# Two convolution layers: two input buffers, and sums of squares issued group by group

## The reference, cut to what matters

```python
def _hconv(x, w, b):
    return _project(_expmap0(_conv3x3(_logmap0(x), w, b)))
def _hbn(x, gamma, beta): ...      # log map, batch norm, exp map, project
out = _hconv(out_of_group_norm, w1, b1)   # first conv_layer
out = _hbn(out, g1, beta1); out = _hrelu(out)
out = _hconv(out, w2, b2)                 # second conv_layer
```

## Time and profile before

| | us |
|---|---|
| median of 3 runs | 12048.74 (12042.55 to 12057.85) |
| the profiled execution, whole | 12020.56 |
| its span, first to last instruction | 12018.7 |
| PE / DVE / ACT busy | 9492.6 (79%) / 9408.9 (78%) / 8396.4 (70%) |

### The profile page before, as it was taken

The page is one execution under the profiler, slowest core; times in us unless marked ns, Lnnn a source line. Parts: engine busy times, 40 slices in busy tenths (PEclk is TensorE's granted clock), DMA queues, the critical chain, the costliest instruction groups (busy, mean ns, idle before and its releaser), DMA issues. The chain is left out here.

```text
span 12018.7 us, 360844 instructions
## 1 busy us (share of the span) xinstructions
PE 9492.6 (79%) x152226; PEld 4623.4 (38%) x152226; DVE 9408.9 (78%) x10971; ACT 8396.4 (70%) x5579; POOL 298.0 (2%) x132
## 2 busy tenths in 40 slices
PE   0888778885657799868888888888888888887787
PEld 0333223333435666533333333333333333333444
DVE  6677656657776666579999999999999999998776
ACT  0555455555531133279999999999999999998777
POOL 0000000000004500000000000000000000000000
PEclk9999999997879899989999999999999999998899
DMA  7888788886642244355555555555555555554555
GB/s 265 236 239 239 208 228 246 244 229 243 269 195 64 69 153 153 127 100 105 104 102 108 102 106 104 107 102 105 102 109 101 107 101 107 104 107 75 178 176 162
DMA packets 1165596, 1796.78 MB, mean 149 GB/s; under 512 B 124832, under 2 KB 929824, under 8 KB 1094048
## 3 DMA queue, kind: packets, MB, share of 16 engines
q1 hardware_dynamic: 1164320, 1777.49, 58.1%
HBM read 701.15 MB, written 402.65 MB: 92 GB/s over the span
## 5 line engine op out<-in xcount | busy, mean ns | idle before, releaser
L1886 DVE SCALAR_TENSOR_TENSOR grown_ex<-ratio,ex 128x2048 f32<-128x2048 f32 x1024 | 2330.8, 2286 | 250.9 <-PE out L2019 107.4
L2019 PE MATMUL out<-ex,kan_basis 32*32 32x512 f32 x32768 | 1451.1, 654 | 637.8 <-DVE z L1868 359.6
L1764 ACT ACTIVATE ex<-ex 128x2048 f32<-128x2048 f32 x1024 | 1925.8, 1899 | 4.1
L2019 PE MATMUL out<-grown_ex,kan_basis 32*32 32x512 f32 x32768 | 1563.8, 645 | 51.7 <-DVE grown_ex L1886 50.8
L547 PE MATMUL conv<-uc,w 128*32 128x512 f32 x12288 | 1442.8, 611 | 21.0 <-DMA uc<-u 21.0
L1760 ACT ACTIVATE ex<-kin,offset 128x2048 f32<-128x2048 f32 x512 | 1013.2, 1991 | 68.8 <-PE out L2019 60.5
L456 ACT ACTIVATE v<-conv,cb 128x512 f32<-128x512 f32 x512 | 350.5, 684 | 789.8 <-PE conv L547 786.4
L2019 PEld LDWEIGHTS out<-ex,kan_basis 32*32 32x32 f32 x32768 | 396.6, 107 | 1113.5 <-issue 1045.1
L2019 PEld LDWEIGHTS out<-grown_ex,kan_basis 32*32 32x32 f32 x32768 | 541.3, 107 | 673.5 <-issue 582.4
L2138 DVE TENSOR_TENSOR d<-xt 128x2313 f32<-128x2313 f32 (+2 forms) x256 | 622.1, 2494 | 215.3 <-PE acc L2195 215.0
L2195 PE MATMUL acc<-d,weights 32*32 32x512 f32 x16384 | 667.1, 632 | 113.3 <-issue 109.6
(11 more groups left out here) (284 smaller groups left out, 17527.2 us busy)
## 6 DMA issues: line engine op xcount, KB each, us to landing
uc<-u SPq DMA_DIRECT2D x2048, 129.0 KB, 2.8
xt<-in_x SPq DMA_DIRECT2D x128, 1024.0 KB, 7.3
t<-v SPq DMA_DIRECT2D x128, 1024.0 KB, 5.8
back_k<-ku SPq DMA_DIRECT2D x1024, 128.0 KB
xt<-in_x SPq DMA_DIRECT2D x32, 2048.0 KB, 7.8
xt<-t SPq DMA_DIRECT2D x64, 1024.0 KB, 7.6
tt<-t SPq DMA_DIRECT2D x64, 1024.0 KB, 10.8
x<-x SPq DMA_DIRECT2D x64, 1024.0 KB, 4.9
```

The lines of the kernel that those rows point to most:

```text
L1764: a.activation(ex[:, j], ex[:, j], ACT.Exp, scale=-1.0).then_inc(exps, 1)
L1886: v.scalar_tensor_tensor(grown_ex[:, j % 2], ratio[:], LARGEST, ex[:, j], ALU.min, ALU.mult).then_inc(grown, 1)
L2019: last = m.matmul(out[rows(i), g, :], k["kan_basis"][rows(g), kind - 1, n, :], base[rows(g), cols(i)], start=(n == 0), stop=(n == BASES - ...
```

## The change

- `xt` gets a second buffer. The load of band `n+1` is issued in round `n`, where that of band `n` was; it waits for the same count of `normed` and `squared` as before. Band 0 is loaded ahead of the rounds. Semaphores `loaded` are split by parity.
- ACT does `square(n, 0)` and `square(n, 1)` earlier: between the evacuations of groups 1, 2 and 3 of half 0 instead of behind them.
- PE does `sum_squares(n)` ahead of `fill_u(n-1, 0)`, no longer ahead of `fill_u(n-1, 2)`.
- `sum_out` is cut into one piece for each group `k`: 2 blocks, two of the four column quadrants, instead of 8 blocks. A piece stands behind the convolution of the next group. `sqv` is four banks, one for each `k`, instead of two halves.
- The convolution of group 0 of half 0 moves from the start of round `n+1` to the end of round `n`, between groups 3 of half 1's convolution and the last piece of `sum_out`. Its evacuation moves with it. `roots` waits for the last piece.
- Some small tiles of DVE are overlaid to make room, and with that the wait for `spread_u` stands earlier in `factors_u`.
- The order of DVE and of SP is as before, apart from that.

```diff
-        xt = sb("xt", [P, HALVES, HALO, COLS])
+        xt = sb("xt", [P, 2, HALVES, HALO, COLS])
-        sqv = sb("sqv", [P, HALVES, TILE])
+        sqv = sb("sqv", [P, 4, BANK])
...
-            def load(r):
+            def load(r, parity):
                 for h in range(HALVES):
-                    wait_both(sp, normed, 2 * (r - 1) + h + 1, squared, 2 * (r - 1) + h + 1)
+                    wait_both(sp, normed, 2 * (r - 2) + h + 1, squared, 2 * (r - 2) + h + 1)
...
+            load(0, 0)
             def round_(n, parity):
-                if exists(n):
-                    load(n)
+                if exists(n + 1):
+                    load(n + 1, 1 - parity)
...
             def evacuate(r, parity, h, groups):
                 if groups[0] == 0:
                     wait_past(act, stored[parity][h], 8 * (r - parity))
                     wait_past(act, measured[h], r - 1)
-                    wait_past(act, summed_out, 2 * (r - 1) + h + 1)
                 for k in groups:
+                    wait_past(act, summed_out, (2 * r + h) * 4 + k - 3)
                     act.wait_ge(conv_ready, (2 * r + h) * 4 + k + 1)
...
             def round_(n, parity):                      # ACT
                 if exists(n - 2):
-                    evacuate(n - 2, parity, 0, (0, 1))
+                    evacuate(n - 2, parity, 0, (1,))
+                if exists(n):
+                    square(n, parity, 0)
                 if first and exists(n - 1):
                     logarithms(n - 1)
                 if exists(n - 2):
-                    evacuate(n - 2, parity, 0, (2, 3))
+                    evacuate(n - 2, parity, 0, (2,))
                 if exists(n):
-                    square(n, 0)
-                    square(n, 1)
+                    square(n, parity, 1)
                 if exists(n - 2):
+                    evacuate(n - 2, parity, 0, (3,))
                     evacuate(n - 2, parity, 1, (0, 1))
...
                     evacuate(n - 2, parity, 1, (3,))
+                if exists(n - 1):
+                    evacuate(n - 1, 1 - parity, 0, (0,))
...
+            def sum_out(r, h, k):
+                if h == 0 and k == 0:
                     wait_past(pe, read, r + 2)
+                pe.wait_ge(evacuated, (2 * r + h) * 4 + k + 1)
+                for i in range(2):
+                    b = BAND * h + 4 * (k // 2) + k % 2 + 2 * i
...
             def round_(n, _):                           # PE
                 if exists(n - 2):
-                    convolve(n - 2, 0, (0, 1))
+                    for k in (1, 2, 3):
+                        convolve(n - 2, 0, (k,))
+                        sum_out(n - 2, 0, k - 1)
                 if exists(n - 3):
                     fill_out(n - 3, 0)
                 if exists(n - 2):
-                    convolve(n - 2, 0, (2, 3))
+                    convolve(n - 2, 1, (0,))
+                    sum_out(n - 2, 0, 3)
+                if exists(n):
+                    sum_squares(n)
                 if exists(n - 1):
                     fill_u(n - 1, 0)
                 if exists(n - 2):
-                    convolve(n - 2, 1, (0,))
+                    convolve(n - 2, 1, (1,))
+                    sum_out(n - 2, 1, 0)
                 if exists(n - 1):
                     fill_u(n - 1, 1)
                 if exists(n - 2):
-                    convolve(n - 2, 1, (1,))
-                if exists(n):
-                    sum_squares(n)
+                    convolve(n - 2, 1, (2,))
                 if exists(n - 1):
                     fill_u(n - 1, 2)
                 if exists(n - 2):
-                    convolve(n - 2, 1, (2,))
-                    sum_out(n - 2, 0)
+                    sum_out(n - 2, 1, 1)
                 if exists(n - 3):
                     fill_out(n - 3, 1)
                 if exists(n - 2):
                     convolve(n - 2, 1, (3,))
-                    sum_out(n - 2, 1)
+                    sum_out(n - 2, 1, 2)
+                if exists(n - 1):
+                    convolve(n - 1, 0, (0,))
+                if exists(n - 2):
+                    sum_out(n - 2, 1, 3)
```

More of the change, by code:

```diff
@@ L345, in sem @@
             return net.sem(local, name)
-        loaded, uc_loaded, measured = ([sem(f"{k}{h}") for h in range(2)] for k in ("loaded", "uc_loaded", "measured"))
-        stored = [[sem(f"stored{parity}{h}") for h in range(2)] for parity in range(2)]
+        uc_loaded, measured = ([sem(f"{k}{h}") for h in range(2)] for k in ("uc_loaded", "measured"))
+        loaded, stored = ([[sem(f"{k}{parity}{h}") for h in range(2)] for parity in range(2)] for k in ("loaded", "stored"))
         ready = sem("params")
@@ L361, in rounds @@
                 round_(n, n % 2)
-            with eng.Fori(2, BANDS // 2) as pair:
+            with eng.Fori(2, BANDS // 2 - 1) as pair:
                 for parity in range(2):
                     round_(pair * 2 + parity, parity)
-            for n in range(BANDS, BANDS + 5):
+            for n in range(BANDS - 2, BANDS + 5):
                 round_(n, n % 2)
@@ L495, in sum_squares @@
                     last.then_inc(summed_u, 1)
[L497 to L498 removed]
+            def sum_out(r, h, k):
+                if h == 0 and k == 0:
                     wait_past(pe, read, r + 2)
[L500 to L502 removed]
+                pe.wait_ge(evacuated, (2 * r + h) * 4 + k + 1)
+                for i in range(2):
+                    b = BAND * h + 4 * (k // 2) + k % 2 + 2 * i
                     q4 = QUAD * (b % 4)
[L504 removed]
+                    last = m.matmul(pc[q4:q4 + QUAD, 1, :], c["ones"][:, b // 4, :], sqv[:, k, COLS * i:COLS * i + COLS],
                                     start=(b < 4), stop=(b >= HALVES * BAND - 4), tile_position=(0, q4))
```

69 lines of the change are left out of this document (32 added, 37 removed).

## The result

| | before | after |
|---|---|---|
| median of 4 runs each, us | 12045.65 (12033.58 to 12057.85) | 12286.3 (12271.1 to 12288.09) |
| span of the profiled execution | 12018.7 | 12286.2 |
| start of the layer behind the two convolutions | 2742.6 | 3116.3 |
| round of the first / second convolution layer | 37.4 / 36.5 | 44.25 / 41.5 |

The account below looks back on a forecast made before the run. Chains of handovers, no full engine or DMA, bound each round. Rounds 5.3 and 5.5 us longer, times 31, add 335 us to 12020.6, giving 12356; 28 more for the median gives 12385 us, range 12200 to 12560.

Parts of the forecast that it names:

- The mechanism: Convolution layers: group 0 queued ahead of the last piece puts half 0's `uc` regroup, 12.8 us, into the chain through `roots`.
- the hold: ACT's first evacuation of half 1 waits for `measure(n-4, 1)`; PE stands 2.3 us before its piece, slot 1 behind it.
- The walk: Step-by-step timing of one round from the read of `roots` to the next: 41.1 us first layer, 40.4 second, before clock loss.
- The rival without a hold: ACT not held by the measurement, slot 1 starts 2.35 us earlier: 146 us less, 12240; chance 0.1.
- The clock: Behind PE's 4.4 us wait for `uc` the clock drops, costing 1.6 us a round in both layers, counted once.
- a bound outside the sum: Second clock loss behind the 2.3 us pause before half 1's piece: 99 us more, 12485; with dear pieces, chance 0.14.
- The pieces: Eight `sum_out` pieces on PE at 0.5 us each, six of them in the loop.
- the low end: Pieces at 0.22 us if the next group fills idle quadrants: 104 us less, 12280; chance 0.08.
- The sum of the layers: Rounds 5.3 us longer in the first and 5.5 in the second convolution layer, times 31 rounds: 335 us.
- The untouched layers: Layers behind the two convolutions: no change in their time was priced.
- The rivals for faster and for no change: Faster: waits go, regroup doesn't replace them, 11910, chance 0.06. No change: gains and loop cancel, 12050, chance 0.04.
- break-even: Loop is shorter than before's round only if `u_done` comes under 21.2 us behind `roots` in the first layer, 20.2 second.

Follow-up runs that it names:

- e1: Changed kernel with the convolution of group 0 of half 0 and its evacuation back at the start of the next round: 12162.05 us, ratio 1.0109 to before.
- x8: x5 with group 0 of half 0 and its evacuation put back at the end of the round, ahead of the last `sum_out` piece: 11965.64 us, ratio 0.9939.
- e2: Changed kernel with the second part of `measure(n-4, 1)` on DVE moved ahead of `take_u` slot 0: 12121.31 us, ratio 1.0072 to before.
- p2: Kernel before with the last pass of the loop over bands written out behind the loop, same work and order: 11907.94 us, ratio 0.9893.
- x5: e1 with the slots one group earlier and ACT's squares and PE's `sum_squares` moved later, two input buffers and pieces kept: 11760.05 us, ratio 0.9769 to before.
- x7: x5 with before's single `xt` buffer and its waits instead of two buffers: 11801.78 us, ratio 0.9803 to before.

## Why the prediction was right, point by point

**The mechanism, right, with one loop missing.** Half 0's regroup came into the chain, as forecast, and PE waits for `uc` 4.5 and 4.1 us once a round (forecast 4.4). The chain was drawn through `roots`. e1 cut exactly that link and won 2.6 us in the first layer and 0.2 in the second, where 5.0 were to be explained. What lengthens the rounds of both layers is the way from group 0 to `u_done` in PE's list: in the first 23.2 us before and 31.7 after, in the second 19.5 and 28.6. Before's way had a pause that no row has shown so far, ahead of `fill_out`:

```profile
815.39 1.15 PE L512 MATMUL spread<-factor_out,c_sel 32*128 32x256 f32 x16 [1.73 <-DVE factor_out L602]
```

In the first layer, one more convolution group came into the way (2.6 us), `sum_squares` (2.3), the hold (2.5), ACT's wait at 825.80 (1.3), six pieces (2.0), group 0 at half clock (2.0 more, 811.42 to 816.14 with its piece) and slot 1 with its piece at half clock (1.4). Out of it went the pause for `factor_out` (1.7), the one for `factor_u` (2.3) and that one's loss of clock (1.6): 8.5, as the rows give.

That the size came out right is in part luck: the walk followed PE's list from `roots` on, so it priced nearly the same instructions as the loop without `roots`. The link through `roots` itself binds in x8.

**The walk.** First layer, from `roots` at 816.37:

| step | forecast | measured |
|---|---|---|
| slot 0 on PE | 16.5 | 16.5 |
| second part of the measurement ends | 21.2 | 21.4 |
| piece behind the hold starts | 22.5 | 22.9 |
| SP's first transfer | 24.95 | 26.75 |
| group 0 of the next band | 37.75 | 39.7 |
| next `roots` | 42.7 | 44.6 |

Of the excess of 1.9 us, 0.4 arise ahead of the piece and 1.4 between it and SP. That is the clock, below.

**The hold by the measurement, right.** Forecast 2.3 us, measured 2.53 (839.25). e2 took it away and won 2.6 in both layers. `fill_u`'s slot 1 and with it `u_done` stood behind this wait, as drawn. The rival without a hold is refuted.

**The clock, one loss too few in the first layer.** The granted clock in single microseconds of the same round:

```profile
838.00:839.00 1.00, 0.00 (x0) 0.00 (x0) 0.11 (x1) 1.00 (x2) 0.00 (x0) 0.95 0.00 0
839.00:840.00 1.00, 0.75 (x4) 0.19 (x4) 0.00 (x0) 1.00 (x3) 0.00 (x0) 0.50 0.00 0
...
856.00:857.00 1.00, 0.91 (x8) 0.27 (x12) 0.00 (x0) 0.00 (x0) 0.00 (x0) 0.50 0.86 201
```

It falls to 0.50, the level of 1.2 GHz, behind the pause of 4.6 us, as forecast, and also behind the 2.53 us before the piece. There the piece takes 1.07 us instead of 0.63 and slot 1 2.09 instead of 1.15: 1.4 us more, in the loop. This stood in the prediction as a bound outside the sum. Slot 1 was slow in 19 of 26 rounds of the first layer. It explains most of the way from 42.7 to 44.25.

In the second layer the clock falls behind this pause as well, but later, mostly on the group behind slot 1, when `u_done` no longer waits for PE:

```profile
2032.20 0.62 PE L510 MATMUL pc<-sqv,c_ones 128*32 128x256 f32 x4 [2.54 <-ACT sqv L459]
2032.76 1.35 PE L518 MATMUL spread<-factor_u,c_sel 32*128 32x256 f32 x16
2034.05 4.21 PE L553 MATMUL conv<-uc,w 128*32 128x512 f32 x24
```

The loss behind the long pause was priced once at 1.6 us. From the start of group 0 to the read of `roots` are 4.55 to 6.20 us in after, on average 5.0 and 5.1 in the two layers, and 3.26 in x8, where group 0 starts behind a pause of 0.2 at full clock: 1.8 and 1.9 us lost, between 1.3 and 2.9 in single rounds. In the second layer every fifth or sixth round takes 42.9 us and the others 41.1 to 41.8; the mean is 41.5.

**The pieces, over-priced.** Forecast 0.5 each, with 0.22 as the low end. In a dense run (2010.71 to 2019.42, three groups of 2.6 and four pieces) they cost (8.71 - 7.8) / 4 = 0.23; behind a wait 0.55 (825.80 to 826.35). Of the six in the first layer's loop two stand behind a wait: some 2.0 us in all, not 3.0. That the idle quadrants take the next group's work fits this, and the timeline shows both overlaid (its ends are modelled).

```profile
2010.71 0.38 PE L510 MATMUL pc<-sqv,c_ones 128*32 128x256 f32 x1
2010.71 0.62 PE L553 MATMUL conv<-uc,w 128*32 128x512 f32 x1
2010.71 0.59 PE L510 MATMUL pc<-sqv,c_ones 128*32 128x256 f32 x3
```

In the second layer slot 0 came 14.45 us behind `roots` instead of 15.8. Of these 1.4 us four cheap pieces are 1.1, and the rest is a slip of the walk: it starts group 1 at `roots`, while PE starts it when the last piece ends, 0.23 us earlier (2011.13 against 2011.36). At SP's first transfer 0.8 of it is left (23.46 instead of 24.25), and at the next `roots` 0.5, 41.5 instead of 42.0.

**The sum of the layers.** Forecast 5.3 and 5.5 us more a round, 335 in all. Measured 6.8 and 5.0, and the convolutions end 373.7 us later. The sentence that the rounds of both layers would be almost equal was wrong: they differ by 2.8. Slot 0 comes 2.0 us later in the first layer (16.48 against 14.45), where a piece waits 1.3 us for ACT and the factors are no earlier, instead of 0.7, and most of the rest is the second loss of clock, which falls into the loop only there.

**The untouched layers, costed at nothing.** That step failed. Behind the convolutions before took 12018.7 - 2742.6 = 9276.1 us and after 9169.9, 106 us less: the window layer 56, the pattern layer 55. So the total rose by 267.5 and not by 374. The forecast lies 99 us above the measured median: the convolutions were costed 39 us too low, the other layers 106 too high, and the 28 us between profiled execution and median, added on top, weren't there in after (12288.1 profiled, 12286.3 median), which makes 30. So the forecast rise of 339 us (12385 - 12045.65) stands against a measured one of 241, though the convolutions themselves were forecast within 39. p2 shows that such a gain comes without any change of work. Against p2, whose later layers are as quick as after's, after is 378 us slower (12286.3 - 11907.94), which is the price of its schedule.

**The rivals for faster and for no change, refuted.** The waits for the input went, as the rule of the Trainium skill ("Trainium Kernel Development and Optimization", Best Practices) lets one expect, but the regroup took their place, and the buffer by itself was worth 0 and 1 us a round (x5 against x7): the trace agrees with the rule on the waits and not on the time. `u_done` came 26.65 us behind `roots` in the first layer (843.12 - 816.37, less 0.1), against a break-even of 21.2. In the second it came about 23.4 behind, against 20.2; there before's 19.1, which the prediction doesn't give, lay below that point, so that only the added work on PE decided. The DMA share was 0.69 and 0.72, near the 0.75 forecast.

## What to carry to other kernels

In a pipeline on engines that take their lists in order, find every loop that runs from an instruction through a DMA back to the same instruction a round later, and write down its length beside the round: a move that puts one group, one sum and one wait ahead of the signal that starts the DMA costs their full length as soon as the slack (here 1.4 us in one layer and 4 in the other) is used up. Put what starts the transfer first and what nobody waits for last; here that order, with the same work, made a round 8.5 and 7.4 us shorter than in after and 1.7 and 2.3 shorter than in before, where the added buffer gave at most 1 us of 35. And before a gain or loss of about 1% is laid to an edit, look at a layer that the edit doesn't touch.

## What was not expected of the hardware

- Untouched layers moved the whole by 1.07% (p2) when only one loop pass ahead of them was written out; 32 more small matmuls ahead of them gave 62 us, 64 cost 0.15%. Why is open.
- A pause of 2.53 us before two small matmuls (four instructions) had the clock at 0.50 behind it and cost 1.4 us, against 1.3 to 2.9 behind one of 3 to 4.6 us. Behind the 1.31 us at 825.80 the next slot took its usual 1.15.
- A small group on two quadrants (four instructions) costs 0.23 us when the next group follows at once, and 0.55 behind a wait; the large one, of 16 instructions on four, took 0.89.
